# The opening of an attention stage in another order: norm and turns of the first chunk ahead of keys and values, value fills spread over the slots

## The reference

```python
x = x + mamba(layernorm(x))                      # a selective scan, 512 channels, 16 states
# cross-attention to the context, 16 heads of 16 features
q = (layernorm(x) @ Wq.T + bq)                   # per token
k, v = ctx @ Wk.T + bk, ctx @ Wv.T + bv          # per context row
q = rope(q, position)                            # q1*cos - q2*sin, q2*cos + q1*sin; only q is turned
p = softmax(q @ k.T / 4)                         # over the 77 rows of the token's sequence, per head
x = x + (p @ v) @ Wo.T + bo
# 8 experts, the best 2 of each token, weighted: down(up(h) * gelu(gate(h))), h = layernorm(x)
x = x + experts(layernorm(x))
```

## Time and profile before

| | us |
|---|---|
| median of 3 runs | 2127.41 (2124.16 to 2128.25) |
| the profiled execution's own time | 2127.51 |
| its span | 2125.7 |
| first load of attention issued | 917.41 |
| first value fill starts on TensorE | 935.06 |
| first maxima of the loop on DVE | 983.00 |

### The profile page before, as it was taken

How to read it: one execution, slowest core, us unless ns; L and a number is a source line. 1 busy time by engine, 2 the same in 40 slices (tenths; PEclk the granted TensorE clock), 3 DMA queues, 4 the chain that set the end, 5 groups by cost and what they waited for, 6 DMA issues and landing times. The chain is left out here.

```text
span 2125.7 us, 29061 instructions
## 1 busy us (share of the span) xinstructions
PE 1899.4 (89%) x10714; PEld 1538.6 (72%) x10714; DVE 1173.8 (55%) x1664; ACT 1086.3 (51%) x2118; POOL 1044.9 (49%) x712
## 2 busy tenths in 40 slices
PE   6889999999999998866999983799999999999998
PEld 2667777777777777654666652688888888888887
DVE  4889998999899988734656546411111111111111
ACT  3898989898989898603666650111111111111111
POOL 1687878787878787605555521322222222222121
PEclk8999999999999999978999995999999999999999
DMA  4021212121212120040000017534343434343441
GB/s 126 22 61 41 69 42 71 40 71 40 71 41 71 31 71 31 21 127 10 21 30 31 21 40 257 219 106 146 102 146 104 144 104 144 105 143 107 136 147 18
DMA packets 86637, 176.81 MB, mean 83 GB/s; under 512 B 12593, under 2 KB 57137, under 8 KB 76258
## 3 DMA queue, kind: packets, MB, share of 16 engines
q1 hardware_dynamic: 72834, 156.27, 21.5%
q0 software_dynamic: 13664, 18.69, 5.4%
HBM read 152.52 MB, written 22.41 MB: 82 GB/s over the span
## 5 line engine op out<-in xcount | busy, mean ns | idle before, releaser
L238 POOL TENSOR_TENSOR m_hc_ring<-m_h_ring,m_c_bc 128x1024 f32<-128x1024 f32 x256 | 606.2, 2374 | 122.6 <-DVE m_h_ring L399 104.4
L1533 PE MATMUL e_ps<-e_xT,w 128*128 128x256 f32 (+1 forms) x2560 | 502.3, 357 | 0.8 <-ACT e_xT L1460 0.8
L1533 PEld LDWEIGHTS e_ps<-e_xT,w 128*128 128x128 f32 x2560 | 441.8, 191 | 51.7 <-issue 1.1
L1444 POOL DMA_INDIRECT out<-e_y,ids x71 | 113.3, 1596 | 564.1 <-DVE e_y L1496 478.7
L490 PEld LDWEIGHTS m_ps<-m_ident,m_bxT 128*128 128x128 f32 x2048 | 234.9, 141 | 210.4 <-DVE m_h_ring L399 97.1
L283 ACT ACTIVATE m_a_ring<-m_delta,m_negA 128x512 f32<-128x512 f32 x512 | 366.1, 716 | 39.9 <-DVE m_h_ring L399 39.4
L490 PE MATMUL m_ps<-m_ident,m_bxT 128*128 128x128 f32 x2048 | 320.7, 279 | 61.9 <-DVE m_h_ring L399 56.1
L295 ACT ACTIVATE m_bxT<-m_uT,m_bT 128x512 f32<-128x512 f32 x512 | 364.4, 712 | 0.0
L1487 DVE TENSOR_TENSOR e_hT<-e_gact,e_ps 128x512 f32<-128x512 f32 x142 | 97.7, 688 | 446.4 <-ACT e_gact L1469 446.4
L399 DVE TENSOR_TENSOR_SCAN m_h_ring<-m_a_ring,m_carry,m_ps 128x512 f32<-128x512 f32 x256 | 316.5, 1267 | 27.6 <-ACT m_a_ring L283 13.1
L399 DVE TENSOR_TENSOR_SCAN m_h_ring<-m_a_ring,m_ps 128x512 f32<-128x512 f32 x256 | 303.8, 1208 | 35.5 <-ACT m_a_ring L283 12.2
(11 more groups left out here) (200 smaller groups left out, 2016.8 us busy)
## 6 DMA issues: line engine op xcount, KB each, us to landing
w<-in_gate_up_w SPq DMA_DIRECT2D x80, 1024.0 KB, 6.9
m_c_bc<-c_rows SPq DMA_DIRECT2D x32, 1024.0 KB, 6.0
w<-in_down_w SPq DMA_DIRECT2D x8, 1024.0 KB, 11.7
m_x_in<-in_x SPq DMA_DIRECT2D x8, 512.0 KB, 5.4
m_x_res<-in_x SPq DMA_DIRECT2D x8, 512.0 KB, 6.6
x<-m_x_res SPq DMA_DIRECT2D x8, 512.0 KB, 2.8
t_xa<-x SPq DMA_DIRECT2D x8, 512.0 KB, 3.9
out<-t_xa SPq DMA_DIRECT2D x8, 512.0 KB, 2.9
```

The source lines that it names most:

```text
L238: p.tensor_tensor(hc_ring[:, k % HC, :, :], h_ring[:, n % 2, e:e + 2, :], c_bc[:, n, :].unsqueeze(1).to_broadcast([P, 2, CT]), ALU.mult).t ...
L1444: nc.gpsimd.indirect_dma_start(out=out, out_offset=bass.IndirectOffsetOnAxis(ap=ids[:, tile:tile + 1], axis=0), in_=y[:, s % 2, i, :], in_ ...
L1533: last = t.matmul(gu_bank(s, g, which)[:, f * wide:(f + 1) * wide], w1[:, s % W1_RING, c, lo:lo + P], xT[:, s % 2, c, 0:wide], start=(c == ...
```

## The change

`START = -HT` is a new mark at slot -8. x of chunk 0 becomes the first load that SP issues. ACT loads its Exp and Ln table first. The code of keys, angles and key blocks that stood ahead of the slots is wrapped in functions and called inside the loop: on TensorE keys follow both XT jobs of slot -8, with `consts` waited for at the start of that slot; on ACT key copies and Sin stand at the head of slot -7; on DVE the angles stand at the head of slot -8, the key blocks at the head of slot -7. The ten value fills stand behind the jobs of slots -8, -8, -7, -6, -6, -5, -4, -4, -3 and -2, on TensorE and on DVE. POOL's first masks move to slot -2. Everything from slot -1 on is as before.

```diff
+    START = -HT
+        VALUES_AT = [START + n * (HT - 1) // V_FILLS for n in range(V_FILLS)]
...
         @block.sync
         def _(sp):
+            sp.dma_start(xa[:, 0, :, :], x1c[0]).then_inc(x_loaded, 16)
             for loaded, pairs in (
...
-            sp.dma_start(xa[:, 0, :, :], x1c[0]).then_inc(x_loaded, 16)
...
             pool.wait_ge(consts, 16 * 9)
-            mask_values(0)
             for g in range(FIRST, LAST):
                 c, q = g // HT, g % HT
+                if g == -2:
+                    mask_values(0)
...
         @block.scalar
...
+            a.preload_act_table_set(EXP_LN)
             for g in range(FIRST, LAST):
                 c, q = g // HT, g % HT
+                if g == START + 1:
+                    keys_and_angles()
...
         @block.vector
...
-            dve.wait_ge(consts, 16 * 9)
...
-            for f in range(V_FILLS):
-                values(f)
             for g in range(FIRST, LAST):
                 c, q = g // HT, g % HT
+                if g == START:
+                    angles()
+                    dve.wait_ge(consts, 16 * 9)
+
+                if g == START + 1:
+                    key_blocks()
...
+                for f in range(V_FILLS):
+                    if g == VALUES_AT[f]:
+                        values(f)
...
         @block.tensor
...
-            pe.wait_ge(consts, 16 * 9)
-            pe.wait_ge(k_evac, KD)
-            for f in range(V_FILLS):
+            def values(f):
+                if f == 0:
+                    pe.wait_ge(k_evac, KD)
                 if f >= 4:
                     pe.wait_ge(v_evac, f - 3)
...
             for g in range(FIRST, LAST):
+                if g == START:
+                    pe.wait_ge(consts, 16 * 9)
                 if g == -1:
                     pe.wait_ge(v_evac, V_FILLS)
                     pe.wait_ge(k_blocks, KD * HP)
...
+                if g == START:
+                    keys()
+                for f in range(V_FILLS):
+                    if g == VALUES_AT[f]:
+                        values(f)
```

More of the change, by code:

```diff
@@ L824, in _ @@
             a = nc.scalar
[L825 to L834, removed]
             def root(rstd, chain, log, c, ready):
@@ L864, in head_out, with keys_and_angles @@
                 a.activation(oT[:, h // 2 % 2, h % 2, :], ps[:, O_BANK, :], ACT.Copy).then_inc(o_evac, 1)
+            def keys_and_angles():
+                act.wait_ge(k_consts, N_K)
+                for c in range(KD):
+                    act.wait_ge(k_done, c + 1)
+                    a.activation(kT[:, c, :], ps[:, c, 0:NBR * M], ACT.Identity,
+                                 bias=bk_col[:, c:c + 1]).then_inc(k_evac, 1)
+                act.wait_ge(trig_step, 8)
+                a.activation(sin_t[:], ang[:], ACT.Sin).then_inc(sin_done, 1)
+                act.wait_ge(trig_step, 10)
+                a.activation(cos_t[:], tmp_t[:], ACT.Sin).then_inc(sin_done, 1)
+                a.preload_act_table_set(EXP_LN)
+            a.preload_act_table_set(EXP_LN)
             for g in range(FIRST, LAST):
                 c, q = g // HT, g % HT
+                if g == START + 1:
+                    keys_and_angles()
                 if g % TI == 1 and 0 <= g // TI - 2 < HALVES:
@@ L901, in step @@
                 dve.wait_ge(trig_step, n)
[L903 to L923, removed]
-            dve.wait_ge(consts, 16 * 9)
+            def angles():
+                dve.wait_ge(angle_consts, N_ANGLE)
+                step(v.tensor_copy(pos_f[:], pos_i[:]), 1)
+                step(v.tensor_tensor(ang[:], pos_f[:].unsqueeze(2).to_broadcast([P, NC * TI, HD // 2]),
+                                     inv_freq[:].unsqueeze(1).to_broadcast([P, NC * TI, HD // 2]), ALU.mult), 2)
+                step(v.tensor_scalar(turns[:], ang[:], 1 / TWO_PI, ROUND, ALU.mult, ALU.add), 3)
+                step(v.tensor_scalar(turns[:], turns[:], ROUND, None, ALU.subtract), 4)
+                for n, part in enumerate((C1, C2, C3)):
+                    step(v.scalar_tensor_tensor(out=ang[:], in0=turns[:], scalar=-part, in1=ang[:],
+                                                op0=ALU.mult, op1=ALU.add), 5 + n)
+                step(v.tensor_scalar(ang[:], ang[:], PI_IN, -PI_IN, ALU.min, ALU.max), 8)
+                step(v.scalar_tensor_tensor(out=tmp_t[:], in0=ang[:], scalar=-1.0, in1=ang[:],
+                                            op0=ALU.mult, op1=ALU.min), 9)
+                step(v.tensor_scalar(tmp_t[:], tmp_t[:], np.pi / 2, None, ALU.add), 10)
@@ L926, in values, with key_blocks @@
+            def key_blocks():
+                dve.wait_ge(k_consts, N_K)
+                for c in range(KD):
+                    dve.wait_ge(k_evac, c + 1)
+                    for h in range(HP):
+                        v.tensor_scalar(k_blk[:, c, :, h * M:(h + 1) * M], kT[:, c, :].rearrange("p (b m) -> p b m", m=M),
+                                        mask[:, h:h + 1], None, ALU.mult).then_inc(k_blocks, 1)
             def values(f):
@@ L1012, in _, with keys @@
             t = nc.tensor
[L1013 to L1018, removed]
-            pe.wait_ge(consts, 16 * 9)
-            pe.wait_ge(k_evac, KD)
-            for f in range(V_FILLS):
+            def keys():
+                pe.wait_ge(k_consts, N_K)
+                for c in range(KD):
+                    for n in range(KD):
+                        last = t.matmul(ps[:, c, 0:NBR * M], wk_sb[:, n, c * P:(c + 1) * P], ctx_rep[:, n, :, 0:M],
+                                        start=(n == 0), stop=(n == KD - 1))
+                    last.then_inc(k_done, 1)
+            def values(f):
+                if f == 0:
+                    pe.wait_ge(k_evac, KD)
                 if f >= 4:
```

## The result

| | before | changed |
|---|---|---|
| median | 2126.62 us (4 runs) | 2112.31 us (2109.96 to 2112.70, 4 runs) |
| profiled execution: time, span | 2127.51, 2125.7 us | 2112.57, 2110.8 us |
| first load issued to first maxima | 65.59 us | 50.58 us |
| first maxima to the end | 1142.70 us | 1143.18 us |

The ratio of the runs is 0.9931, interval 0.9919 to 0.9943, which of 2126.6 us is 14.7 us faster (12.1 to 17.2); the medians are 14.3 us apart. The spans differ by 14.9 us. The opening gives 15.0 us, the phase ahead of it happened to end 0.4 us sooner, and the rest of the kernel is 0.5 us longer. That distance was between 1142.45 and 1143.58 us in all twelve profiles of this study, whatever was done to the opening, so 0.5 us more or less is within what profiles of this kernel differ by.

The account below looks back on a forecast made before the run. Attention's loop was taken as bound by TensorE and unchanged, with the opening's hand-overs between four engines to be shortened: -14.25 - 0.5 + 0.3 = -14.45 us, giving 2113.0 us, range 2109.5 to 2117.5.

Parts of the forecast that it names:

- the sum: Step-by-step timeline of the opening, from the wait for nine constants to first maxima: 14.25 us sooner, before corrections.
- the 51.3 us among its signs: Sign to look for: first maxima near 51.3 us after the first load's issue instead of 65.6.
- The load of x and the norm: Start of the opening: x loaded first costs nothing, and 3.8 us of norm leaves the path, covered by bo's load.
- correction (a): Constants' load: x in front leaves the stretch ahead of bo, constants land 0 to 1.4 us sooner; taken as -0.5.
- Keys behind the gate, key blocks before q: After the constants' wait: keys put 4 us on the path, and the first q waits 3.8 us behind key blocks.
- Rotation beside fills: After the second q: POOL's 7.92 us rotation is hidden under TensorE's fills, TensorE being 1.2 us late for it.
- Masks, and DVE's scalar step: Behind the rotation: POOL's masks run 962.8 to 968.7 us, free; DVE's scalar step for chunk 1's norm falls among them.
- correction (b): DVE's scalar step of chunk 1's norm, now among the masks: bounds 0 and +1.0 us, taken as +0.3.
- The exclusion of DVE and POOL: Skill's rule applied to chunk 1's norm beside masks: four scalings could lose 2.4 us if masks ran past 969.6 us.
- The clock did not fall in the wait: Rival: TensorE's clock falls in 3.1 us idle before the second q, +1.0 to +2.7 us, 2115.0 us; chance 0.30.
- given back by the loop: Rival: the loop loses the opening's gain to missing inputs, 2121 us, or 2127.4 if all is lost; chance 0.08.
- the clock might stay low all through: Rival: the new opening runs at 1.2 GHz throughout, +20.2 us, 2133.2 us; chance 0.05.

Follow-up runs that it names:

- e10: The changed kernel with x of chunk 0 issued behind the keys' and angles' loads as before; median 2114.39 us, ratio 0.9947 to before.
- e5: The changed kernel with key matmuls and ACT's part of keys and angles back under the load; median 2111.48 us, ratio 0.9931 to before.
- e6: As e5, with DVE's 16 key blocks under the load too, behind the angles; median 2105.98 us, ratio 0.9902 to before.
- e2: The changed kernel with all ten value fills together in slot -8, ahead of q; median 2124.87 us, ratio 0.9996 to before.
- e3: The changed kernel with DVE's 16 key blocks two slots later, beside POOL's rotation; median 2116.97 us, ratio 0.9958 to before.
- e4: The changed kernel with 16 more products of the same shape ahead of the key blocks in DVE's queue; median 2118.20 us, ratio 0.9965 to before.
- e8: The changed kernel run again without any edit; median 2113.70 us, ratio 0.9938 to before.
- e7: As e6, with the gate waiting for six constants, the other three counted apart and waited for in slot -1; median 2105.29 us, ratio 0.9906 to before.
- e9: As e7, with ACT's two Sin and their table loads moved behind the copies of the turned x; median 2104.36 us, ratio 0.9893 to before.

## Why the prediction was right, step by step

The mechanism was right: the rotation went under the fills, the norm under the load, and keys and key blocks came out of their cover. The time was closer (0.7 us) than the parts were: the opening is 50.6 us where the sum gives 51.1 (the 51.3 us among its signs left the corrections out), the phase ahead ended 0.4 us sooner and the rest is 0.5 us longer. With the runs of the changed kernel up to 2.7 us apart, that the distance is under 1 us is luck.

Times from the gate to each step, in us:

| step | predicted | measured |
|---|---|---|
| first value fill | 6.9 | 6.8 |
| DVE adds the first q | 16.1 | 15.8 |
| TensorE's wait before the second q | 3.1 | 2.56 |
| second q | 16.9 | 16.6 |
| rotation starts | 19.8 | 19.5 |
| turn of q | 29.0 | 28.7 |
| first scores | 32.4 | 31.9 |
| first maxima | 33.7 | 33.2 |

**The load of x and the norm.** Right that it costs nothing and that the norm leaves the path. It said too much of the order: correction (a) took 0.5 us for a gate that a filled hole would bring forward. The gate came 0.26 us sooner, and with x back in its place (e10) it is 0.13 us off. That the hole closes was wrong, for it is as deep in the changed kernel's row as in the row of before; what was gained at the gate is within what repeated runs of one kernel differ (17.39 and 17.14).

**Keys behind the gate, key blocks before q.** Right, and shown singly: bringing the keys back gives 2.8 us (e5), the blocks 2.9 us more (e6). The sum had written beside them 4 us for the keys and 3.8 us for q's wait behind the blocks (3.1 us of it idle on TensorE, 2.56 measured), so both were sized too large. The first fill does start 4.1 us sooner in e5, but then more of the fills run at the low clock (4.81 us for two, 3.72 in the changed kernel); and of q's wait behind the blocks TensorE filled a part with fill 2.

**Rotation beside fills.** Right: the turn of q waited for nobody but TensorE, and without the spreading (e2) 14.15 us come back. But e2 also shows that norm and turns ahead are worth at most 0.9 us by themselves, 0.5 of which is a gate that came sooner: what they save is paid out again for keys and blocks. The gain of the change is the spreading. That it needs the early q follows from the order of the queues; no run spread the fills without it.

**Masks, and DVE's scalar step.** The masks ended at 967.7 us, ahead of POOL's next work, so free as said. The step took 0.44 us (1.12 before), 0.7 us ahead of the next addition: correction (b) was 0 and not +0.3. The exclusion of DVE and POOL was worth weighing, but in another place: in e3 it costs DVE 7.4 us for 16 blocks where POOL is busy. The change's own place for the blocks, ahead of the rotation, avoids it.

**The rivals.** The clock did not fall in the wait; e4 shows that the price was right (2.2 us), had the wait been longer. Nothing was given back by the loop, in any of twelve profiles. That the clock might stay low all through did not come near: 0.92 in the mean from the gate to the first maxima.

## What to carry to other kernels

Put the work that makes the longest engine hand-over (here q, for a rotation on GpSimd) ahead of independent work that was to come anyway, and check in each in-order queue what it then stands behind: here norm and turns ahead were worth at most 0.9 us without the spread fills, and 15 with them. What used to hide under a load should stay under it: keys and key blocks pushed behind the gate cost 5.6 of a possible 20.6 us. Don't put a row of float32 `tensor_scalar` into VectorE's queue beside a busy GpSimd: in e3 it took 12.13 us instead of 4.71.

## What the runs showed of the hardware

- Beside GpSimd's `tensor_tensor` on SBUF, VectorE's `tensor_scalar` on float32 got through once for each GpSimd instruction, and VectorE bore nearly all of it (e3): 0.37 us became 0.73 in the median and up to 1.42, GpSimd's rotation steps stayed at 1.26 us, its masks went from 0.62 to 0.69 us. The Trainium skill, "SBUF — State Buffer", section "Who interferes with whom", states such an exclusion, for the whole of the instruction that issues first. The trace agrees for VectorE, the later one: each of the three blocks issued 0.02 us behind a rotation step ended 0.17 to 0.18 us behind that step's end.
- TensorE's clock kept 2.4 GHz through one wait of 2.56 us between dense stretches (four profiles: changed, e5, e8, e10) and fell in waits of 4.29 us (e2), 6.09 (e3) and 7.20 (e4). In e7 it fell with waits of 1.75 and 2.13 us that had only 0.66 us of work between them.
- Work that starts sooner need not meet the high clock sooner: behind the gate the clock came up after 5.2 us in the changed kernel (4.9 to 5.6 in the other kernels that wait for nine constants), 7.7 us in e7 and 6.9 us in e9, although e9 had done 4.47 us of key matmuls just ahead.
